# Gathered features of layer 0 as three 16-bit pieces, with 16-bit choices

## What is computed

```
h       = relu(layernorm(x))
out_deg = count of edges by src;  in_deg = count of edges by dst
hs      = h * out_deg ** -0.5                    # by row, degrees at least 1
agg     = segment_sum(hs[src], dst)              # 128 columns
esum    = segment_sum(edge_attr @ We + be, dst)  # 128 columns of edge features
conv    = agg @ W * in_deg ** -0.5 + b
x       = x + conv + (h @ W + b) / (in_deg + 1) + esum / in_deg
```

## Time and profile before

| | |
|---|---|
| median of 3 runs | 7222.97 us (7200.09 to 7244.32) |
| span of the profiled execution, first to last instruction | 7221.2 us |
| DVE busy in it | 3856.8 us |
| TensorE busy, matmuls | 4312.1 us |
| GpSimd busy | 4096.8 us |

### The profile page before, as it was taken

How to read it: one execution, slowest core, us unless ns; L and a number is a source line. 1 busy time by engine, 2 the same in 40 slices (tenths; PEclk the granted TensorE clock), 3 DMA queues, 4 the chain that set the end, 5 groups by cost and what they waited for, 6 DMA issues and landing times. The chain is left out here.

```text
span 7221.2 us, 86037 instructions
## 1 busy us (share of the span) xinstructions
PE 4312.1 (60%) x19030; PEld 3495.4 (48%) x19030; DVE 3856.8 (53%) x11927; ACT 1462.0 (20%) x3928; POOL 4096.8 (57%) x4194
## 2 busy tenths in 40 slices
PE   4577777846656565795666666333344446556565
PEld 4466666635555555443444444233333345555554
DVE  7344444446666556745555555244444446556665
ACT  4122222212222222361111111000000112222222
POOL 1566666646666565006666665666666556555653
PEclk9877767666666666897888888555655566676766
DMA  2433333323333334164444445122222433333333
GB/s 49 125 99 101 100 100 101 100 89 105 106 108 108 105 108 87 64 279 140 130 136 128 136 129 117 52 55 61 59 56 59 72 100 107 110 113 105 113 115 64
DMA packets 426871, 738.64 MB, mean 102 GB/s; under 512 B 100571, under 2 KB 280628, under 8 KB 419797
## 3 DMA queue, kind: packets, MB, share of 16 engines
q0 software_dynamic: 173296, 436.67, 23.0%
q1 hardware_dynamic: 244484, 289.62, 12.3%
q10 hardware_dynamic: 8592, 6.82, 0.4%
HBM read 613.74 MB, written 120.20 MB: 102 GB/s over the span
## 5 line engine op out<-in xcount | busy, mean ns | idle before, releaser
L1619 POOL DMA_INDIRECT xh<-pair_d,src_i x1658 | 1653.2, 997 | 1181.9 <-issue 457.1
L2630 POOL DMA_INDIRECT l2e_rows<-msg_d,msg_i x829 | 807.1, 974 | 744.7 <-POOLq L61 316.8
L986 POOL DMA_INDIRECT l0e_rows<-node_d,src_i x832 | 793.9, 954 | 465.0 <-issue 220.6
L841 POOL DMA_INDIRECT l2f_rows<-msg_d,msg_i x829 | 787.0, 949 | 428.4 <-issue 231.2
L1141 PE MATMUL l0e_ps<-l0e_rows,l0e_sel 128*128 128x256 f32 x1664 | 787.1, 570 | 304.1 <-issue 187.3
L875 PE MATMUL l2f_ps<-l2f_rows,l2f_sel 128*128 128x128 f32 x1664 | 403.8, 409 | 597.2 <-DVE xh L906 482.6
L2748 PE MATMUL l2e_ps<-l2e_rows,l2e_sel 128*128 128x256 f32 x1664 | 485.8, 424 | 423.2 <-DVE l2e_sel L2842 406.4
L875 PEld LDWEIGHTS l2f_ps<-l2f_rows,l2f_sel 128*128 128x128 f32 x1664 | 359.1, 304 | 671.3 <-issue 409.6
L2807 DVE TENSOR_TENSOR l_acc<-l_acc,l2e_ps 128x256 f32 x832 | 349.2, 420 | 511.5 <-DMA node_d<-l1t_queries 347.7
L1206 DVE TENSOR_TENSOR early_acc<-early_acc,l0e_ps 128x264 f32 x832 | 356.6, 429 | 470.7 <-PE l0e_ps L1142 181.6
L906 DVE TENSOR_TENSOR xh<-xh,l2f_ps 128x128 f32 x832 | 238.2, 286 | 676.3 <-DMA tb_raw<-edges_d,starti 466.7
(11 more groups left out here) (454 smaller groups left out, 8155.1 us busy)
## 6 DMA issues: line engine op xcount, KB each, us to landing
l0e_rows<-in_edge_attr_dram SPq DMA_DIRECT2D x832, 64.0 KB
msg_d<-l1t_queries SPq DMA_DIRECT2D x50, 1024.0 KB, 3.9
l1te_local<-local_d SPq DMA_DIRECT2D x52, 512.0 KB
l2e_local<-local_d SPq DMA_DIRECT2D x52, 512.0 KB
l3te_local<-local_d SPq DMA_DIRECT2D x52, 512.0 KB
xh<-pair_d,src_i POOLq DMA_INDIRECT x1658
msg_d<-l2e_msg SPq DMA_DIRECT2D x50, 512.0 KB
l0e_rows<-node_d,src_i POOLq DMA_INDIRECT x832
```

Of the source, the lines that this page charges most:

```text
L841: pool.indirect_dma_start(rows[:, t % R, :], None, table, bass.IndirectOffsetOnAxis(index[:, t:t + 1], 0)) \
L986: pool.indirect_dma_start(rows[:, t % R, 0:D], None, table, bass.IndirectOffsetOnAxis(g.src_i[:, t:t + 1], 0)).then_inc(gathered[t % R], 16)
L1619: pool.indirect_dma_start(rows[:, t % R, :], None, g.pair_d, bass.IndirectOffsetOnAxis(g.src_i[:, t:t + 1], 0)).then_inc(gathered[n % RG], 16)
L2630: pool.indirect_dma_start(rows[:, t % R, :], None, table, bass.IndirectOffsetOnAxis(index[:, t:t + 1], 0)).then_inc(gathered[t % R], 16)
```

## The change

The chunk of scaled features is split on its way to `node_d`: ScalarE copies it to 16 bits (the first piece), DVE subtracts that piece from the chunk, ScalarE copies the remainder to 16 bits (the second), DVE writes what is then left in 16 bits (the third). `node_d` has rows of 3 x 128 16-bit numbers, 768 bytes, where it had 512. In the pass the gathers fill `near`, the edge features go to a tile `far` of their own, still f32. For each tile TensorE multiplies the 16-bit choice `narrow` by the 16-bit columns of relations, then by each of the three pieces, added up in the bank, and the f32 choice `sel` by `far`. The wait of `choose` for earlier sums stands ahead of its first half, as TensorE now reads `narrow`. Three scratch tiles move to a buffer that is idle here.

```diff
--- before.py
+++ after.py
@@ -328,13 +328,16 @@
         nsrc, rstd2, shift2 = (st.sb(k, [P, NW]) for k in ("nsrc", "rstd2", "shift2"))
         junk = scratch[:, 0:4 * D].rearrange("p (b f) -> p b f", b=4)
         hn = scratch[:, 4 * D:24 * D].rearrange("p (b w f) -> p b w f", b=4, w=5)
+        spare = scratch[:, 24 * D:24 * D + 3 * 960].bitcast(BF16)
+        pieces = [spare[:, 1920 * b:1920 * (b + 1)].rearrange("p (w j f) -> p w j f", w=5, j=3) for b in range(3)]
+        pieces.append(g.mask[:, :, :, :].rearrange("p a b c -> p (a b c)")[:, 0:1920].rearrange("p (w j f) -> p w j f", w=5, j=3))
         ps = st.ps("ps")
         pt = [st.ps("pt0"), st.ps("pt1")]
         (dv, built, counted, squared, evened, rooted, scaled, normed, asked, answered, scaled2, sent_a, sent_d,
-         laid, turned, taken, keyed, kept, out) = (
+         laid, turned, taken, keyed, kept, out, headed, left, middled, tailed) = (
             sem("tb_" + k) for k in ("dv", "built", "counted", "squared", "evened", "rooted", "scaled", "normed",
                                      "asked", "answered", "scaled2", "sent_a", "sent_d", "laid", "turned", "taken",
-                                     "keyed", "kept", "out"))
+                                     "keyed", "kept", "out", "headed", "left", "middled", "tailed"))
         got = [sem(f"tb_got{k}") for k in range(3)]
         hn_out = [sem(f"tb_hn_out{b}") for b in range(4)]
         BY_ACT = (0, 3, 6)
@@ -367,12 +370,9 @@
                     sp.dma_start(g.key[0:n, b, :], view(g.keys_d.tensor, P + b * P * P - 1, [[P, n], [1, P + 2]])) \
                         .then_inc(g.keys_in, 16)
                 for k in range(K):
-                    if k in BY_ACT:
-                        sp.wait_ge(sent_a, 5 * (BY_ACT.index(k) + 1))
-                    else:
-                        sp.wait_ge(sent_d, len([j for j in range(k + 1) if j not in BY_ACT]))
+                    sp.wait_ge(tailed, k + 1)
                     sp.dma_start(g.node_d[k * 5 * P:(k + 1) * 5 * P, :].rearrange("(w p) f -> p w f", p=P),
-                                 hn[:, slot[k], :, :]).then_inc(hn_out[slot[k]], 16)
+                                 pieces[slot[k]].rearrange("p w j f -> p w (j f)")).then_inc(hn_out[slot[k]], 16)
                 for b in range(4):
                     sp.wait_ge(hn_out[b], 16 * len([k for k in range(K) if slot[k] == b]))
 
@@ -414,12 +414,32 @@
                 act.wait_ge(asked, 1)
                 nc.scalar.activation(nsrc[:, :], nsrc[:, :], ACT.Sqrt).then_inc(answered, 1)
                 act.wait_ge(scaled2, 1)
-                for k in BY_ACT:
+
+                def scale_rows(k):
                     if turn_of[k]:
                         act.wait_ge(hn_out[slot[k]], 16 * turn_of[k])
                     for v in range(5 * k, 5 * k + 5):
                         nc.scalar.activation(hn[:, slot[k], v % 5, :], g.x[:, v * D:(v + 1) * D], ACT.Relu,
                                              bias=shift2[:, v:v + 1], scale=rstd2[:, v:v + 1]).then_inc(sent_a, 1)
+
+                def take_head(k):
+                    if k in BY_ACT:
+                        act.wait_ge(sent_a, 5 * (BY_ACT.index(k) + 1))
+                    else:
+                        act.wait_ge(sent_d, len([j for j in range(k + 1) if j not in BY_ACT]))
+                    nc.scalar.copy(pieces[slot[k]][:, :, 0, :], hn[:, slot[k], :, :]).then_inc(headed, 1)
+
+                def take_middle(k):
+                    act.wait_ge(left, k + 1)
+                    nc.scalar.copy(pieces[slot[k]][:, :, 1, :], hn[:, slot[k], :, :]).then_inc(middled, 1)
+
+                for k in range(K + 1):
+                    if k in BY_ACT:
+                        scale_rows(k)
+                    if k < K:
+                        take_head(k)
+                    if k >= 1:
+                        take_middle(k - 1)
 
             @block.tensor
             def _(pe):
@@ -492,13 +512,31 @@
                 c.step(nc.vector.tensor_tensor(rstd2[:, :], rstd[:, :], nsrc[:, :], ALU.mult))
                 nc.vector.tensor_tensor(shift2[:, :], shift[:, :], nsrc[:, :], ALU.mult).then_inc(scaled2, 1)
                 dve.wait_ge(normed, NW)
-                for k in range(K):
-                    if k not in BY_ACT:
-                        if turn_of[k]:
-                            dve.wait_ge(hn_out[slot[k]], 16 * turn_of[k])
-                        nc.vector.tensor_tensor(
-                            hn[:, slot[k], :, :], g.h[:, 5 * k * D:5 * (k + 1) * D].rearrange("p (w f) -> p w f", f=D),
-                            nsrc[:, 5 * k:5 * (k + 1)].unsqueeze(2).broadcast_to([P, 5, D]), ALU.mult).then_inc(sent_d, 1)
+
+                def scale_rows(k):
+                    if turn_of[k]:
+                        dve.wait_ge(hn_out[slot[k]], 16 * turn_of[k])
+                    nc.vector.tensor_tensor(
+                        hn[:, slot[k], :, :], g.h[:, 5 * k * D:5 * (k + 1) * D].rearrange("p (w f) -> p w f", f=D),
+                        nsrc[:, 5 * k:5 * (k + 1)].unsqueeze(2).broadcast_to([P, 5, D]), ALU.mult).then_inc(sent_d, 1)
+
+                def take_from(k):
+                    dve.wait_ge(headed, k + 1)
+                    nc.vector.tensor_tensor(hn[:, slot[k], :, :], hn[:, slot[k], :, :], pieces[slot[k]][:, :, 0, :],
+                                            ALU.subtract).then_inc(left, 1)
+
+                def take_tail(k):
+                    dve.wait_ge(middled, k + 1)
+                    nc.vector.tensor_tensor(pieces[slot[k]][:, :, 2, :], hn[:, slot[k], :, :], pieces[slot[k]][:, :, 1, :],
+                                            ALU.subtract).then_inc(tailed, 1)
+
+                for k in range(-1, K + 1):
+                    if 0 <= k < K:
+                        take_from(k)
+                    if k >= 1:
+                        take_tail(k - 1)
+                    if 0 <= k + 1 < K and k + 1 not in BY_ACT:
+                        scale_rows(k + 1)
 
 
 def make_masks(nc, g, dve, c):
@@ -939,11 +977,11 @@
     acc, table = g.acc0, g.node_d
     DVE_, ACT_, SP_ = mybir.EngineType.DVE, mybir.EngineType.Activation, mybir.EngineType.SP
     with Stage(nc, "l0e") as st:
-        rows = st.sb("rows", [P, R, 2 * D])
+        near, far = st.sb("near", [P, R, 3 * D], BF16), st.sb("far", [P, R, D])
         sel = st.sb("sel", [P, 2, G, P])
         narrow = st.sb("narrow", [P, 2, P, G], BF16)
         numbers, dloc16 = st.sb("numbers", [P, P, G], BF16), st.sb("dloc16", [P, T], BF16)
-        of_rel = st.sb("of_rel", [P, 2, G, RELS])
+        of_rel = st.sb("of_rel", [P, 2, G, RELS], BF16)
         w0, b0 = st.sb("w0", [P, 2, D]), st.sb("b0", [P, 2, D])
         w1, bq = st.sb("w1", [P, 3 * D]), st.sb("bq", [P, D])
         deg, both, part, more, has = (st.sb("deg", [P, 1]), st.sb("both", [P, 2]), st.sb("part", [P, 2]), st.sb("more", [P, 1]),
@@ -953,8 +991,8 @@
         z, zt, wraw = zz[:, 0:2, :], zz[:, 2:4, :], zz[:, :, :].rearrange("p k f -> p (k f)")
         total, less, var = st.sb("total", [P, 1]), st.sb("less", [P, 1]), st.sb("var", [P, 1])
         rstd, shift = st.sb("rstd", [P, 1]), st.sb("shift", [P, 1])
-        junk, hc, ht = st.sb("junk", [P, D]), st.sb("hc", [P, D]), st.sb("ht", [P, D])
-        vk, prod = st.sb("vk", [P, 2 * D]), st.sb("prod", [P, D])
+        junk, hc, ht = g.coef[:, 3 * D:4 * D], st.sb("hc", [P, D]), st.sb("ht", [P, D])
+        vk, prod = g.coef[:, 0:2 * D], g.coef[:, 2 * D:3 * D]
         ps = [st.ps(f"ps{b}") for b in range(B)]
         pzt, pz, ph, pv = st.ps("pzt"), st.ps("pz"), st.ps("ph"), st.ps("pv")
         gathered = [sem(f"l0e_g{r}") for r in range(R)]
@@ -983,7 +1021,7 @@
                 for t in range(T):
                     if t >= R and t % G == 0:
                         pool.wait_ge(summed, t - R + G)
-                    pool.indirect_dma_start(rows[:, t % R, 0:D], None, table,
+                    pool.indirect_dma_start(near[:, t % R, :], None, table,
                                             bass.IndirectOffsetOnAxis(g.src_i[:, t:t + 1], 0)).then_inc(gathered[t % R], 16)
 
             @block.sync
@@ -1012,7 +1050,7 @@
                         for r in range(R):
                             e0 = first[r]
                             reach(sp, summed, R * (i - 1) + r + 1)
-                            sp.dma_start(rows[:, r, D:2 * D], features[bass.ds(e0, P), :]).then_inc(loaded[r], 16)
+                            sp.dma_start(far[:, r, :], features[bass.ds(e0, P), :]).then_inc(loaded[r], 16)
                             if r == 8:
                                 keep_turned(i - 6)
                                 store(i - 6)
@@ -1138,8 +1176,11 @@
                     reach(pe, added, R * i + r - B + 1)
                     pe.wait_ge(gathered[r], 16 * (i + 1))
                     pe.wait_ge(loaded[r], 16 * (i + 1))
```

(11 more changed lines are left out.)

## The result

| | before | after |
|---|---|---|
| median, 14 runs each | 7222.93 us (7200.09 to 7250.3) | 7268.38 us (7256.11 to 7291.23) |
| ratio of after to before, 95% interval | | 1.0064 [1.0052, 1.0076] |
| span of the profiled execution | 7221.2 us | 7270.9 us |

The change costs 45 us, 0.64% (by the interval 38 to 55). I forecast a time 13 us under that of before.

A forecast was written before the change was run, and what follows sets the result against it. Late sums while GpSimd gathers, not TensorE's work, were taken to hold the pass. 7221 - 33 (pace) + 24 (tables) = 7212, given as 7210 us; own range 7150 to 7260, 8-in-10 range 7090 to 7270.

The forecast's parts named there:

- The stage's pace after that: Layer 0's pass: 1.44 us a tile instead of 1.48, 33 us gained over 832 tiles; ends 190 gained, 17 lost.
- The tile: TensorE's work per tile in the pass: 0.44 us at 2.4 GHz and 0.89 at 1.2, where it took 0.65 and 1.28.
- The rival without a TensorE saving: Strided weights load slowly, the pass's tile stays 1.28 us and only the tables count: 7245 us; chance 0.12.
- The tables: Before the pass: splitting ten chunks takes 41.8 us instead of 17.6 up to the first gather, 24 us lost.
- TensorE setting the pace: TensorE bounds the pass, so its saving counts until GpSimd binds: 7055 to 7130 us, about 7090; chance 0.28.
- The slower one: Slow weight loads and a 1.2 GHz clock throughout the pass: 7405 us, a lesser form 7295; chance 0.12.
- sums that reach VectorE several microseconds after TensorE's last record: Sign that the forecast is right: in the pass, sums still reach the vector engine this late.
- the first gather near 232: Sign that the forecast is right: the pass's first gather near 232 us; beyond 245 would show it wrong.
- GpSimd's count: Sign in the pass: gathers per 1100 us rise from 744 only to 755 to 775; over 800 means TensorE was the bound.
- TensorE's busy time: Sign that the forecast is right: it falls by a quarter or more in the pass.
- within 1%: Whole kernel's time within about 72 us of no change: chance 0.57, against faster 0.30 and slower 0.13.

The follow-up runs named there:

- e1: Changed kernel with one of the three pieces multiplied, 768-byte gathers kept: ratio 1.0039 to the kernel before, pass 1251.4 us.
- e14: Kernel before with 16-bit relation columns, their matmul written four times instead of once: ratio 1.0022, pass 1282.6 us on a slow chip.
- e17: Kernel before with gathered rows of 768 bytes, the added columns multiplied by nobody: ratio 1.0021, pass 1275.2 us on a slow chip.
- e13: Kernel before with one 32-bit matmul of 264 columns a tile in place of two: ratio 1.0058, pass 1327.2 us on a slow chip.
- e16: Changed kernel with a 384-column memset on GpSimd behind every gather of the pass: ratio 1.0062, pass 1301.6 us on a slow chip.
- e11: Kernel before with only the relation columns made 16-bit and multiplied by the 16-bit selection: ratio 0.9983, pass 1247.0 us.

## Why the prediction was wrong

*Which step failed.* "The stage's pace after that", the 33 us gained. I took 1.44 us a tile from two stages with a light TensorE, 1.425 and 1.49, and measured 1.493 in the steady part, where it was 1.478 (1.520 and 1.506 over the whole pass). The stages had shown me rightly that TensorE's load isn't the bound, but not what the bound would be here. With e1 as a check, a light TensorE in this very pass gives 746 gathers in 1100 us, 1.475, not 1.44; so a light TensorE alone doesn't make the quicker stage's 1.425, and what sets a stage's pace had to be tried, not borrowed. The term was -33 and should have been +11. Those 44 us and the 21 in layer 2, less 5 elsewhere, are the distance from 7210 to the profiled 7271.

*The tile: its sum right, its parts not.* In weight loads of the changed kernel, first where the granted clock is 0.50, then where it is 1.00:

```profile
299.88 0.15 PEld L1180 LDWEIGHTS l0e_ps<-l0e_of_rel,l0e_narrow 128*128 128x128 bf16 x1
...
300.76 0.15 PEld L1180 LDWEIGHTS l0e_ps<-l0e_of_rel,l0e_narrow 128*128 128x128 bf16 x1
...
881.66 0.11 PEld L1180 LDWEIGHTS l0e_ps<-l0e_of_rel,l0e_narrow 128*128 128x128 bf16 x1
...
881.78 0.20 PEld L1182 LDWEIGHTS l0e_ps<-l0e_near,l0e_narrow 128*128 128x128 bf16 x3
...
881.92 0.30 PEld L1183 LDWEIGHTS l0e_ps<-l0e_far,l0e_sel 128*128 128x128 f32 x2
...
882.14 0.11 PEld L1180 LDWEIGHTS l0e_ps<-l0e_of_rel,l0e_narrow 128*128 128x128 bf16 x1
```

A tile takes 0.88 us at 1.2 GHz (predicted 0.89) and 0.48 at 2.4 (predicted 0.44). Of the 0.48 the record of 8 columns has 0.12, where I put 0.025, the three pieces 0.14, where I put 0.20, and the 32-bit pair 0.22, where I put 0.21. That two errors nearly cancel is luck. The rival without a TensorE saving falls, since its tile was 1.28 us. The Trainium skill ("TensorE: Matmul & The Clock Gate", Weight-path perf modes — Fast Weight Load (FWL) and DoubleRow) says that weights which are not f32 load faster when there are 128 of them, packed or strided; here, with 128 rows and a step of four elements, the trace agrees: the pieces follow each other 0.05 us apart, the 32-bit pair 0.11. The strided record of the earlier trace rows, 107 ns each, differs in its 125 rows and in its step of 16, and no run shows which of them mattered.

*The tables: right.* The first gather at 231.03 against 232, a round of 3.1 us against 3.5, and one wait for a store that I hadn't counted.

*Left out.* That two matmuls more might cost anything while TensorE is idle: I costed TensorE by time alone. And the 21 us of layer 2, for which the sum had no term.

*The rivals.* TensorE setting the pace falls with the 737 gathers. The slower one (slow loads at 1.2 GHz) has the right sign by another road: the loads are fast and the clock stayed at 0.70; e1 shows that the clock does fall, to 0.56, when the tile is lighter still, with a pass no longer for it. Of the signs, sums that reach VectorE several microseconds after TensorE's last record came true (617.66), and the first gather near 232; GpSimd's count, 755 to 775 by the forecast, fell to 737, and TensorE's busy time fell by 23%, just short of a quarter. That the range, up to 7270, just held the 7268 is luck: 21 us of the way there are a loss in layer 2 for which it had no case. Of the chances, "within 1%" came true.

*What stays open.* Of the 50 us between the two profiled executions the 23 of the tables have a cause that was measured; the others have a place and no cause. Open is what passes some 1.50 us a tile and no faster. Open is whether the 11 us of the pass are the two matmuls (e1, e14) or partly the rows (e17). And the 21 us of layer 2's first gather stage, which has the same code: on the quick chips the four kernels with the old tables take 1,233 to 1,238 us from first to last gather there, and the six profiled with the new tables 1,246 to 1,255, so it goes with the change. On the one slow chip that had both kinds (e13 to e16) it is 1,257 and 1,259 with the old tables, 1,266 and 1,267 with the new; the two other slow chips had one kind each. Layer 1's gathers scatter by 40 us between kernels without such an order (1,340 to 1,379), which warns against reading much into ten.

No kernel here that does all the work beats the one before by more than 0.2%. The best, e11, takes the cheapest part of the change alone: 0.9983 [0.9970, 0.9997].

## What to carry to other kernels

Before shortening an engine's work, look for the stage's rate: if it hardly moves when that engine's load is doubled or halved, and the engine upstream stops and starts, the stops are the difference of two rates and not a cost of their own. Spacing the upstream engine's work out until the stops vanish brackets the rate, here with one short filler instruction. A wait for several things is read from the code as well as from the view, and finished work is counted against its readers, one by one, before a delay is given a number. And work added ahead of a pipeline, like the 23 us in the tables here, is paid in full whatever the pipeline then does. Where code that nobody changed scatters by 0.5%, a difference of 0.2% in the whole is no evidence on a part.

## What the runs showed of the hardware

- Gathers of 128 rows issued by GpSimd as fast as it can, 1.25 us apart, got through at 1.47 to 1.51 us a tile in the steady part of the pass. At 1.34 us apart the rate was the same. At 1.55 us apart the waits for sums fell from 217 to 6 us in 1100. Without gathers a tile took 0.95 us.
- A gather's last packet begins 1.4 us after the end of GpSimd's instruction (median of the changed kernel's pass), also while other engines wait for late news.
- While GpSimd runs ahead, sums done at 610.13 to 612.03 were not noticed before 617.66; in the tables VectorE noticed at 82.83 what TensorE had finished by 66.88.
- The mean granted clock moved with the load at nearly one and the same pace of the pass: 0.56, 0.70 and 0.83 of 2.4 GHz with one piece, three and six multiplied.
- Chips differ by 0.7% in the same stage (1,180.5 and 1,189 us), by 1.0% in the same pass (1264.4 and 1276.8) and by 2.2% in layer 3's gathers (1,382 and 1,412 on average), more than some of the differences sought here.
